# A macaron block on one core: first feed-forward and keys as one stage, v's bias moved, and two PSUM areas in the second factorisation

## The reference

```
x = x + 0.5 * ffn(layernorm(x), W1, b1, W2, b2)
x = x + attn(layernorm(x), Wq, bq, Wk, bk, Wv, bv, Wo, bo)
x = x + 0.5 * ffn(layernorm(x), W1, b1, W2, b2)
```

## Time and profile before

| | us |
|---|---|
| median of 3 runs (1189.35 to 1190.5) | 1189.91 |
| the profiled execution, its own time | 1187.86 |
| its span, from first to last instruction | 1186.1 |
| PE busy (share of the span) | 967.0 (82%) |
| DVE busy | 812.4 (68%) |
| ACT busy | 528.6 (45%) |
| POOL busy | 274.3 (23%) |
| mean granted clock of PE, as a share of full speed | 0.889 |
| ffn1's load of x, from issue to landing | 3.5 |
| store of aT, and of uT, in keys, from issue to landing | 5.2, 5.3 |

### The profile page before, as it was taken

One profiled execution on the slowest core, in us unless ns is written; L12 is line 12 of the kernel. 1 busy time (PEld: TensorE's weight loads), 2 busy tenths in 40 slices (PEclk: granted clock), 3 DMA queues, 4 the chain that ended last, 5 costly groups with the idle time before them and its releaser, 6 DMA issues. The chain is left out here.

```text
span 1186.1 us, 29797 instructions
## 1 busy us (share of the span) xinstructions
PE 967.0 (82%) x11492; PEld 733.3 (62%) x11492; DVE 812.4 (68%) x2598; ACT 528.6 (45%) x1083; POOL 274.3 (23%) x222
## 2 busy tenths in 40 slices
PE   3899999956886798879895164784799479999998
PEld 1466666646773476666793154663799446666666
DVE  6677777647976988959367797976344457776674
ACT  4677777724783222312232022111122167777774
POOL 3344333403430000000000000000455333433440
PEclk9899999987997878879898575887799789999999
DMA  4344433324776624335451000055777334334451
GB/s 140 83 115 112 123 107 106 90 96 156 249 243 163 184 75 116 83 86 148 127 168 36 2 3 3 4 145 117 195 237 226 130 83 107 107 106 112 124 115 57
DMA packets 186123, 138.73 MB, mean 117 GB/s; under 512 B 86562, under 2 KB 170787, under 8 KB 185379
## 3 DMA queue, kind: packets, MB, share of 16 engines
q1 hardware_dynamic: 172962, 112.10, 35.5%
q10 hardware_dynamic: 13056, 25.17, 5.9%
HBM read 65.87 MB, written 46.14 MB: 94 GB/s over the span
## 5 line engine op out<-in xcount | busy, mean ns | idle before, releaser
L340 DVE TENSOR_TENSOR ffn_h_rest<-ffn_ps_h,ffn_h_high 128x512 f16<-128x512 f32 x256 | 175.9, 687 | 126.4 <-ACT ffn_ps_h L437 119.4
L486 PE MATMUL ffn_ps_y<-w_ternary,ffn_h_high 128*128 128x256 f16 x1024 | 236.8, 274 | 7.5 <-DVE ffn_h_rest L340 7.4
L486 PE MATMUL ffn_ps_y<-w_ternary,ffn_h_rest 128*128 128x256 f16 x1024 | 236.7, 274 | 0.0
L472 PE MATMUL ffn_ps_h<-ffn_xT_high,w_ternary 128*128 128x512 f16 x512 | 197.9, 386 | 20.9 <-DMA ffn_xT_rest<-ffn_xn_rest 19.0
L436 ACT ACTIVATE ffn_h_high<-ffn_ps_h,b_columns 128x512 f16<-128x512 f32 x256 | 178.9, 699 | 79.3 <-PE ffn_ps_h L472 79.0
L472 PE MATMUL ffn_ps_h<-ffn_xT_rest,w_ternary 128*128 128x512 f16 x512 | 197.7, 386 | 0.0
L437 ACT ACTIVATE ffn_ps_h<-ffn_ps_h,b_columns 128x512 f32<-128x512 f32 x256 | 172.5, 674 | 0.0
L1587 POOL TENSOR_TENSOR out_v_over_d<-out_v,out_dcol 128x512 f32<-128x512 f32 x16 | 16.6, 1039 | 513.3 <-DMA out_v<-v_scratch 479.3
L486 PEld LDWEIGHTS ffn_ps_y<-w_ternary,ffn_h_high 128*128 128x128 f16 x1024 | 100.6, 98 | 46.3 <-DVE ffn_h_rest L340 9.7
L486 PEld LDWEIGHTS ffn_ps_y<-w_ternary,ffn_h_rest 128*128 128x128 f16 x1024 | 100.6, 98 | 32.9 <-issue 0.6
L472 PEld LDWEIGHTS ffn_ps_h<-ffn_xT_high,w_ternary 128*128 128x128 f16 x512 | 51.1, 100 | 64.2 <-DMA ffn_xT_rest<-ffn_xn_rest 20.7
(11 more groups left out here) (163 smaller groups left out, 1668.4 us busy)
## 6 DMA issues: line engine op xcount, KB each, us to landing
ffn_x<-in_x SPq DMA_DIRECT2D x16, 512.0 KB, 3.5
x_scratch<-ffn_x_out ACTq DMA_DIRECT2D x16, 512.0 KB, 2.9
keys_x<-x_scratch SPq DMA_DIRECT2D x16, 512.0 KB, 4.4
aT_scratch<-keys_aT SPq DMA_DIRECT2D x16, 512.0 KB, 5.2
inv_aT<-aT_scratch SPq DMA_DIRECT2D x16, 512.0 KB, 4.4
out_x<-x_scratch SPq DMA_DIRECT2D x16, 512.0 KB, 4.8
x_scratch<-out_x_out ACTq DMA_DIRECT2D x16, 512.0 KB, 5.3
ffn_x<-x_scratch SPq DMA_DIRECT2D x16, 512.0 KB, 3.3
```

Source lines behind the costliest of these rows:

```text
L340: nc.vector.tensor_tensor(hl[st.s][:, f], ps_h[f % 4][:], hh[st.s][:, f], ALU.subtract).then_inc(hl_done, 1)
L472: ins = nc.tensor.matmul(ps_h[f % 4][:], c.w1[:, d, f * P:(f + 1) * P], part[st.s][:, :, d], start=(k == 0), stop=(k == 2 * DC - 1))
L486: ins = nc.tensor.matmul(ps_y[t % 2][:], part[st.s][:, f, t * P:(t + 1) * P], c.w2[:, f], start=(f == 0 and part is hh), stop=(f == FC - 1 ...
```

## The change

It has three parts.

1. `feed_forward` for ffn1 and `keys` become `feed_forward_keys`, one stage of 21 steps (16 blocks, and five to drain), all written out with no loop. The keys of block k take x1 from the tile in which the feed-forward leaves it (`xo`), so nothing is loaded back; x1 is still stored for the later stages. x is read and x1 written with a partition's four rows 128 rows apart (four pieces of 1 KB) in place of four rows together (4 KB), so that a tile of 128 rows is a chunk. The work on block k is put at fixed places f of steps k + 1 to k + 4. `ps_h` has three banks in place of four, since `ps_t` (which takes both the turned a and the turned u), `ps_k` and `ps_p` need one each.
2. v's bias no longer enters by a matmul in `qv`; POOL adds it to v in place in `outputs`, ahead of the scaling, from a tile loaded there.
3. In "ldl" `work` becomes two areas of four banks, used in turn; a fill waits for what last used its own area, and where a fill reads what ACT copies out of the other, for that copy (`free`, `emptied_of`). "inv" keeps one area.

```diff
-        ps_h = [psum(f"ps_h{i}", [P, BLOCK]) for i in range(4)]
+        ps_h = [psum(f"ps_h{i}", [P, BLOCK]) for i in range(3)]
+        ps_t = psum("ps_turned", [P, HC, P])
...
+            @block.vector
+            def _(v):
...
+                def row_stats(k, t):
+                    v.wait_ge(xo_done, BT * k + t + 1)
+                    nc.vector.bn_stats(a_bn[:, t], xo[k % 2][:, t]).then_inc(a_bn_done, 1)
...
+                for n in range(NALL):
+                    on(n + 1, normalise)
+                    for f in range(FC):
+                        on(n, rest, f)
...
+                        if n == 1 and f == 3:
...
+                            units()
+                        if f == 0:
+                            on(n - 2, normalise_out)
+                        if 1 <= f <= HC:
+                            on(n - 4, prefix, f - 1)
+                        if f == 2:
+                            on(n - 3, invert)
+                        if f in (2, 4, 6):
+                            on(n - 1, finish, (f - 2) // 2)
+                            on(n - 1, row_stats, (f - 2) // 2)
+                        if f == 6:
+                            on(n + 2, stats)
+                        if f == 7:
+                            on(n - 2, add_bias)
+                    on(n - 1, finish, BT - 1)
+                    on(n - 1, row_stats, BT - 1)
+                    on(n - 1, aggregate)
+
+            @block.gpsimd
+            def _(pool):
...
+                for n in range(NALL):
+                    on(n - 2, rsqrt_out)
+                    on(n + 1, split)
+                    on(n - 3, root)
+                    on(n, add_bias)
+                    on(n + 2, rsqrt)
+
+            @block.scalar
+            def _(act):
...
+                for n in range(NALL):
+                    for f in range(FC):
+                        on(n, gelu, f)
+                        if f == 0:
+                            on(n + 1, high)
+                            on(n - 3, squares)
+                        if f == 1:
+                            on(n - 4, copy_uT)
+                        if f == 2:
+                            on(n - 2, store)
+                        if f == 3:
+                            on(n - 2, copy_aT, 0)
+                            on(n - 3, scale_u)
+                        if f == 5:
+                            on(n - 2, copy_aT, 1)
...
+            @block.tensor
+            def _(pe):
...
+                def turn_a(k, half):
+                    if half == 0:
+                        pe.wait_ge(an_done, k + 1)
+
+                        if k > 1:
+                            pe.wait_ge(uT_done, k - 1)
+                    wait(pe, aT_done, 2 * k + half)
...
+                for n in range(NALL):
+                    for f in range(FC):
+                        on(n, first_product, f)
+                        if f:
+                            on(n - 1, second_product, (f - 1) // 2, (f - 1) % 2)
+                        if f == 2:
+                            on(n - 2, turn_a, 0)
+                        if f == 4:
+                            on(n - 2, turn_a, 1)
+                        if f == 5:
+                            on(n - 2, product, 0)
+                        if f == 6:
+                            on(n - 2, product, 1)
+                        if f == 7:
+                            on(n - 3, turn_u)
+                            on(n - 3, gram)
+                    on(n - 1, second_product, BT - 1, 1)
...
-        work = psum("work", [P, NQ, P])
+        works = [psum(f"work{i}", [P, NQ, P]) for i in range(1 if first else 2)]
...
+        def area(r, what):
+            return works[turn_number[r, what] % len(works)]
...
-                    nc.tensor.matmul(ps_v[:], c.causal[0:1, :], bv[:].unsqueeze(1).to_broadcast([1, HC, H]),
-                                     start=True, stop=False, skip_group_check=True)
...
+                sp.dma_start(bv[:], a["bqkv"][2 * H:].partition_broadcast(P)).then_inc(bv_in, 16)
                 load_rest(Step(0, 0))
...
+                    nc.gpsimd.tensor_tensor(v0[st.s][:], v0[st.s][:], bv[:].unsqueeze(1).to_broadcast(group), ALU.add
+                                            ).then_inc(biased, 1)
+                    pool.wait_ge(biased, st.n + 1)
                     nc.gpsimd.tensor_tensor(vd[st.s][:], v0[st.s][:], dcol[st.s][:].unsqueeze(2).to_broadcast(group),
```

More of the change, by code:

```diff
@@ L216, in feed_forward @@
+def feed_forward(nc, name, src, dst, c):
     x_v = src.rearrange("(n p t) d -> n p t d", p=P, t=BT)
@@ L938, in factorise, with free, emptied_of @@
         fill_number = {key: i for i, key in enumerate(fill_list)}
+        turns = [x for r in range(NW + 1) for x in ([(r, "diagonal")] if r < NW else []) + [(r, f) for f in fills_of(r)]]
+        turn_number = {key: i for i, key in enumerate(turns)}
+        def area(r, what):
+            return works[turn_number[r, what] % len(works)]
+        def free(eng, r, what):
+            before = turns[:max(0, turn_number[r, what] + 1 - len(works))]
+            fills = [fill_number[x] for x in before if x[1] != "diagonal"]
+            taken_of = [x[0] for x in before if x[1] == "diagonal"]
+            if fills:
+                eng.wait_ge(emptied, fills[-1] + 1)
+            if taken_of:
+                eng.wait_ge(taken, taken_of[-1] + 1)
+        def emptied_of(eng, r, what):
+            if (r, what) in fill_number:
+                eng.wait_ge(emptied, fill_number[r, what] + 1)
         def slot(n):
@@ L1152, in next_block @@
                             act.wait_ge(yd_done, 2 * r + 1)
-                        copy(Y[r][:, pr, y(r, cols)], work[:, pr, W:2 * W]).then_inc(y_done, 1)
+                        copy(Y[r][:, pr, y(r, cols)], area(r + 1, "diagonal")[:, pr, W:2 * W]).then_inc(y_done, 1)
                 def empty(r, what):
+                    work = area(r, what)
                     act.wait_ge(filled, fill_number[r, what] + 1)
@@ L1222, in _ @@
             def _(pe):
-                def free(fill):
-                    wait(pe, emptied, fill)
-                    r = fill_list[fill][0]
-                    if r < NW:
-                        pe.wait_ge(taken, r + 1)
                 def done(r, what):
-                    fill = fill_number[r, what]
-                    free(fill)
+                    free(pe, r, what)
+                    emptied_of(pe, r - 1, "panel right" if what == "done right" else "panel")
+                    work = area(r, what)
                     src = ZR if what == "done right" else Z
@@ L1239, in done, with inject @@
                     i.then_inc(filled, 1)
-                def inject(r, src, cols, dst, alone):
+                def inject(work, r, src, cols, dst, alone):
                     for b, q in bank_order():
@@ L1750, in macaron @@
         constants(nc, ctx, c)
[L1751 removed]
         with ExitStack() as own:
[L1753 removed]
+            m.KK = own.enter_context(nc.sbuf_tensor("KK", [P, NP, P], F32))
             m.dinv = own.enter_context(nc.sbuf_tensor("dinv", [P, NP], F32))
             m.knorm, m.uq = (own.enter_context(nc.sbuf_tensor(n, [P, NP], F32)) for n in ("k_norms", "u_dot_q"))
[L1756 removed]
+            feed_forward_keys(nc, a["x"], x1, m, c, a)
+            m.T = own.enter_context(nc.sbuf_tensor("T", [P, NP, P], F32))
             factorise(nc, "inv", m, c, a)
```

708 lines of the change are left out of this document (399 added, 309 removed).

## The result

The changed kernel takes 1201.76 us (median of 4 runs, 1200.05 to 1203.57), the kernel before on the same chip 1189.69 (4 runs): a ratio of 1.0083, with a 95% interval from 1.0060 to 1.0105. It is **slower, by 12 us**, where 4.4 were forecast. The ratio on record is not the quotient of the two medians, which is 1.0101; both lie in the interval, and by the ratio the loss is 10 us. On another chip the pair gave 1.0079 (1.0051 to 1.0107; 1203.68 against 1196.23 us, +7.5 by the medians).

A forecast was written before the change was run, and what follows sets the result against it. ffn1 was taken as PE-bound, keys as bound by no engine, ldl's boundaries by DVE. Fused stage +5.7, bias -2.3 in inv and +1.0 in outputs, areas 0: +4.4 us, 1194 on the median, range 1177 to 1207.

The forecast's parts named there:

- The mechanism of the fused stage: Loop from finish through high and copy_uT to turn_a: PE idles 2.6 us a step, 20.75 us a step.
- step 1: Fused stage, units on DVE within the step: 2.7 us beyond the earlier 53.6, ending at 56.3.
- step 2: Fused stage, no squares, copy_uT, turn_u or u u'; PE waits 0.4 us for normalise_out: 17.05 us.
- step 3: Fused stage, lacking copy_uT: 18.1, 0.4 and 0.45 us, 18.95 us in all.
- steps 4 to 15: Fused stage's steady state: twelve steps of 20.75 us, 249 us.
- step 16: Fused stage's first drain step: second products 7.0, keys 4.2, waiting 2.6, 13.85 us on PE.
- the tail: Fused stage's drain, block 15 alone from its last finish to the next stage: 17.5 us.
- normalise_out, which comes after POOL's root: Fused stage, step 2: 1.8 us from aggregate's start to normalisation, then 1.38; ends at 4.5, PE waits 0.4 us.
- the clock after a wait: Fused stage: 2.6 us of PE idleness a step forecast, with no cost put on a lower clock afterwards.
- up to 2.2 less, I take 1.1: inv, before the last leaf: two bias products fewer shorten DVE's 6.5 us wait for PE by 1.1 us.
- would only move: inv, beside leaf 2: PE stalls without a releaser in the same stretch would shift rather than vanish.
- Fetch was taken as 0: Fused stage, written-out code: fetch stalls put at 0, with 4 us left to the range.

The follow-up runs named there:

- the third link: Changed kernel with POOL's split waiting for a, uT copied a step earlier, and POOL's x plus bias waiting for DVE's eps addition: 0.9879 of the kernel before, 1180.18 us.
- the split-waits kernel: Changed kernel with POOL's split made to wait until DVE has written a: 1201.73 us, one run.
- three links and one area: Kernel before with the fused stage, v's bias still in inv, split and x-plus-bias waits added, uT copied a step earlier: 0.9842 of before, 1173.16 us.

## Why the prediction was right in sign and short in size

**The mechanism of the fused stage was right.** PE waits in every step before `turn_a`, the copy of uT ends that wait, and the step is 20.33 against 20.75 forecast: 6.6 us for 6.7 from finish to turn_a, 13.8 for 13.95 from there on, and the 0.1 added for handovers was not there. Alone, the fused stage cost 5 us where 5.7 were forecast, but errors met in that number: in its trace the stage ended 5.6 later than forecast, "inv" took 6.5 less than before and "ldl" 4.3 more (one execution each, on two chips, so roughly).

**The stage was mis-sized by 4 us** (end at 376.9, forecast 372.7). By the steps: step 1 ended 0.7 late; step 2 took 21.6 where 17.05 was put, **+4.6**, and step 3 20.1 where 18.95 was, +1.2; steps 4 to 15 came 5.0 under; step 16 took 15.1 for 13.85 and the tail 19.0 for 17.5, +2.8. Two steps of the prediction failed.

*The first is "normalise_out, which comes after POOL's root"*: the chain was right, and its last link was priced at the 1.38 us of ffn1's normalisation, beside which POOL waits for ACT. Here POOL's split starts in the middle of it, and it takes 3.18. In steady state the copy of uT hid that; in step 2, which has no such copy, `turn_a` starts 5.1 us after the normalisation where it starts 3.3 after it when the split waits: 1.8 us. In step 3 it cost 0.2: with the split waiting it still took 19.90, and 18.93 only when POOL's x plus bias waited too, so the third link, which the prediction didn't have, was 1.0 of the 1.2 there.

*The second is a term that the prediction put at nothing: the clock after a wait.* It forecast 2.6 us of idleness a step and priced what follows at ffn1's granted clock of 0.98. In steps 2, 10 and 16 PE came back from that wait at the lower clock. Step 16 shows the price alone, since the split-waits kernel has the same wait of 2.44 us there and keeps the higher clock. The turn and the granted clock behind it, first in the changed kernel, then in the split-waits kernel:

```profile
346.94 1.11 PE L667 MATMUL ffn_ps_turned<-ident,ffn_a 128*128 128x128 f32 x4 [2.44 <-DVE ffn_a L421]
...
346.90:350.20 3.30, 3.26 (x16) 2.52 (x17) 2.06 (x9) 1.76 (x5) 0.00 (x0) 0.53 0.00 0
```
```profile
345.50 0.66 PE L669 MATMUL ffn_ps_turned<-ident,ffn_a 128*128 128x128 f32 x4 [2.44 <-DVE ffn_a L421]
...
345.00:348.20 3.20, 2.70 (x25) 2.51 (x26) 2.79 (x12) 1.76 (x5) 0.16 (x1) 1.00 0.00 0
```

Step 16 took 15.12 and 13.64 us (forecast 13.85): 1.5. Step 10 took 1.6 more than its neighbours, and of step 2's 4.6 the clock is 1.6 as well (15.3 us from `turn_a` to the next finish against 13.7). The three come to 4.7 us, more than the 4.2 by which the stage ended late. Which waits the clock falls behind stays open: of the eleven of 2.26 us, in steps 4 to 14, it fell behind one, and step 3, whose wait was 3.12 us, kept the higher clock. Where the waits were short it didn't: with three links and one area PE waited at most 1.3 us at `turn_a` between 60 and 300 us, and came back at the higher clock each time.

The Trainium skill (SBUF — State Buffer, SBUF: two separate sides) says that VectorE, in an instruction of a 2-port mode or with two inputs in SBUF, and GpSimd lock one shared pair of ports, that whichever starts first holds it for the whole instruction, and that the other "fully blocks". By that rule, which the prediction did not weigh, this case's rows read as they stand, if these DVE instructions run in such a mode, which no row names: DVE's float32 tensor_scalar from SBUF waits POOL's instruction out (3.18 for 1.38 us, 2.13 for 0.16). DVE's rows that read PSUM kept their times beside POOL: `rest` at 226.94 and 228.37 in the changed kernel took 0.68 and 0.69.

**v's bias: its gain in "inv" isn't shown, and where the sum came out it was by luck.** In the changed kernel DVE's last two waits fell by what was forecast (6.5 to 5.0, 11.5 to 10.3). But with the bias moved alone they are 6.1 and 12.0, and with the fused stage alone, the bias still in "inv", 1.1 and 10.9. Two rows of the bias alone, then one of the fused stage alone:

```profile
515.90 0.76 DVE L1106 SCALAR_TENSOR_TENSOR inv_panel_over_d<-inv_work,inv_dinv_turned 128x256 f32<-128x256 f32 x2 [6.14 <-PE inv_work L1301]
...
577.25 1.29 DVE L1417 TENSOR_TENSOR gram_Td<-T,dinv 128x512 f32<-128x512 f32 x2 [11.98 <-PEq L948]
```
```profile
522.26 0.76 DVE L1288 SCALAR_TENSOR_TENSOR inv_panel_over_d<-inv_work,inv_dinv_turned 128x256 f32<-128x256 f32 x2 [1.09 <-PE inv_work L1483]
```

These waits move with PE's stalls by as much as the 16 products were said to cost, so the step "up to 2.2 less, I take 1.1" can't be read off them. That the stalls without a releaser "would only move" was written of one stretch; in this execution they stood a boundary earlier, where no slack was, for 4.6 us, and in another execution of the same kernel for 0.8. At outputs the forecast let only the bias tile be late and gave +1.0. In the trace v itself, second in the queue now, was 4.5 us from its issue to POOL's start, against 2.8, and PE's wait grew by 2.0.

**Two areas**: 0 forecast, +1 measured alone with an interval through 0, and PE's wait in "ldl" grown from 38.7 to 59.8 as said. For "inv", which has one area in either version, nothing was expected, and its traces with that code lie at 207.6 us and more; PE's block is written there with some further waits (`emptied_of`), which with one area are already met. That they cost anything isn't shown.

**Fetch was taken as 0** because the fused stage issues little: within that stage this holds (0.7 us of such stalls). What was missed is that new code in front changes the stalls of the code behind it: "inv" ran from 203.2 to 216.4 us. The Trainium skill (Runtime: NRT & Kernel Launch, Instruction fetch mechanics) has sequential fetch hidden; by it fetch would make "inv" neither longer nor shorter in any of these kernels. Its length did change, but whether the stalls are fetches stays open, and with it whether this case disagrees with the page, as the prediction had it: no row names their cause, and the wait before `turn_a`, which the experiment showed to be ACT's, carried the same label.

## What to carry to other kernels

When stages are merged, check who runs beside whom, not only who waits for whom: an instruction priced in one stage may take two or three times as long beside another engine's (a very small one over ten times), and a wait put on the engine with slack can make the kernel faster. When two links end a wait within 0.3 us of each other, the profile's releaser is one of two, and only taking both away shows the gain. A wait that a pipeline has in every step can cost twice, once as idleness and once by the clock that the engine comes back at, so its price is a range and not a number. And a change of 0.5% in one stage of a written-out program has to be measured in the whole that it will stand in, as the untouched stages behind it can move by more.

## What the runs showed of the hardware

- A DVE tensor_scalar on four float32 numbers per partition took 0.16 us alone and 1.05 to 2.13 us beside a POOL instruction on 128x1024, and ended with it. POOL's split took 2.38 us beside DVE's a, and 2.12 behind it.
- After a wait of 2.52 us in step 2 PE came back at the lower of its two clocks (1.2 GHz; the granted clock from 63.3 to 66.5 us is 0.50, before and after it 1.00 and 0.97): a matmul of a first product took 0.63 us there and 0.38 at 67.20. From the timeline of the changed kernel:

```profile
63.33 1.11 PE L667 MATMUL ffn_ps_turned<-ident,ffn_a 128*128 128x128 f32 x4 [2.52 <-DVE ffn_a L421]
64.24 0.63 PE L639 MATMUL ffn_ps_h<-ffn_xT_high,w_ternary 128*128 128x512 f16 x1
...
67.20 0.38 PE L639 MATMUL ffn_ps_h<-ffn_xT_high,w_ternary 128*128 128x512 f16 x1
```

- The same kernel had 18.1 us of PE's stalls without a releaser in "inv" in one execution and 14.2 in another, and took 212.0 and 208.8 us for it.
